# Attention passes of a graph network kernel: fewer semaphore signals from TensorE, weighing moved between the scans and fed from PSUM

## The chip, the cores and the metric

The program runs on one core of a Trainium2 chip. The core has five engines with instruction streams of their own: TensorE (PE; its weight loads are listed apart as PEld), VectorE (DVE), ScalarE (ACT), GpSimd (POOL) and SyncE (SP). They meet at semaphores: an instruction can add to one when it ends ("a signal"), and another engine's instruction can wait until it has reached a value. The metric is the time of one execution in microseconds of the device, lower is better; three runs of the kernel before took 7196.2, 7173.81 and 7191.65 us.

## The reference, cut to what matters

Four layers on a graph with 3125 nodes, 256 features and 53125 edges (25000 drawn, their reverses, and a loop at each node, sorted by destination). The first and the last sum over edges. The second is two GAT layers with 4 heads, the third is three layers of a graph transformer with 8 heads. Both do this for each edge and head (`z` or `V` is the value, `e` the score):

```python
# GAT (two layers): the score is a sum of two per-node numbers
e = leaky_relu(el[src] + er[dst], negative_slope=0.2)
ex = exp(e - segment_max(e, dst)[dst])
out = segment_sum(z[src] * (ex / segment_sum(ex, dst)[dst])[:, :, None], dst)
# graph transformer (three layers): the score is a dot product
scores = sum(Q[dst] * typed(K[src]), axis=-1) / sqrt(32) * mu[edge_type]
e = exp(scores - segment_max(scores, dst)[dst])
agg = segment_sum(V[src] * (e / segment_sum(e, dst)[dst])[..., None], dst)
```

So both need a softmax over the edges of each destination, and a sum weighted by it. Accumulations are in float32.

## The kernel before: how the work is laid out

`attend` (line 672) is called five times: twice for the GAT layers (table `tab_z`, here called the z passes; `dots` is false) and three times for the transformer layers (`tab_kv`, the kv passes; `dots` is true). It takes the sorted edges in chunks of 128 edges, one edge per partition, and 16 chunks make a window. A z pass has 28 windows, the last of them half a window, and a kv pass has 29.

The engines run the same loop over rounds, written out in Python. In round r, parts of windows r, r-1 and r-2 are worked on at once:

- **POOL** issues one indirect DMA per chunk (line 757), which gathers 128 rows of the table into a ring of four windows. Four chunks are a quad. Before a quad, POOL waits until the values that lie at its place have been used: on `s_pp`, which counts finished sums of PE, and in the kv passes on `s_mul` also (lines 748 to 753).
- **SP** loads the destinations of eight chunks at a time, broadcast over the partitions (`oht<-lo_row`, line 741), when `s_q` says that the rows they replace have been used. **ACT** makes one-hot matrices of them (L855, L858), and the other way round for the sums (L864, L869).
- **PE** `qrows` fetches the query rows by multiplying with the one-hot matrix (L785 with three bf16 terms in kv, L779 in z). `T1` (L793) transposes the window's scores; `below` (L797, L798) subtracts the maximum; `ratio` (L802) gets the factor by which earlier sums shrink; after ACT's two exponentials (L881, L882) `T5` (L807) transposes the weights back, and `factor` (L813 to L815) spreads the factor over the partitions. `agg` (L828) sums the weighted values of one unit into a PSUM buffer `pp`: a unit is one chunk in z, with six buffers, and two chunks in kv, with three.
- **DVE** `dot` and `red` make the scores in kv (L931, L936), `leaky` in z (L945, L948, L951). D1, D2, D3 are the segmented maximum, made of scans (L961 to L989). `weigh` (L1010) multiplies a quad of gathered values by the weights, `rescale` (L1000, L1001) multiplies the sum of the current tile by the factor, and `add` (L1018) adds one unit's PSUM buffer to the accumulator.
- **ACT** also copies the weights from PSUM beside the values in the ring (L886, L887, or L889 in z) and the factor to `facs` (L893); in kv it weighs the last two chunks itself (L876).

`T1`, `below`, `ratio`, `T5` and `factor` write to one PSUM bank, `pc`. Semaphores keep all other uses of that bank apart.

Four strings set the order within a round: `ORDER_V_DOTS` and `ORDER_V_SUMS` for DVE in kv and z, `ORDER_T_DOTS` and `ORDER_T_SUMS` for PE. A letter is a step and a number its part: in the V strings W0 to W3 weigh a quad of window r-2, S and R are dot and red of window r, A the adds of window r-2, P the last adds of window r-3, t the rescale, L leaky, B the residual. In the T strings C1 to C5 are T1, below, ratio, T5 and factor of window r-1, G0 to G7 the eighths of agg of window r-2, Q and N the query rows. Nothing reorders them: each engine does its list in order, and waits at its head.

The lines that the steps below refer to most:

```python
# agg, one unit: every unit signals
for c in range(UC):
    last = nc.tensor.matmul(pp[(w * NU + n) % NB][:, 0:W8], oh[...], one(w, UC * n + c, 0, W8), ...)
last.then_inc(s_pp, 1)
# weigh, one quad: values and weights both from the ring in SBUF
ex = span(w, 4 * q, c1, D, D + heads)
nc.vector.tensor_tensor(v, v, bc(ex, 3, D // heads), ALU.mult).then_inc(s_m, 1)
```

## Time and profile before

| | |
|---|---|
| median of three runs | 7191.65 us (7173.81 to 7196.2) |
| the profiled execution's own time | 7153.48 us |
| its span, first to last instruction | 7151.4 us |
| PE busy | 4511.4 us (63%) |
| DVE busy | 3873.4 us (54%) |
| ACT busy | 3586.2 us (50%) |
| POOL busy | 3942.8 us (55%) |
| TensorE clock, mean | 0.769 of full |

The profile is of one execution. "Busy" does not count waiting, branching or the issuing of ordinary DMAs, while POOL's indirect DMAs count for as long as POOL works on them. No engine is busy all the time; the page gives shares over stages of quite different kinds. The five calls of `attend` stand at 1555 to 2273, 2337 to 3052, 3236 to 3972, 4314 to 5052 and 5396 to 6138 us of the span.

### The profile page before, as it was taken

Reading aid. Unit: us, or ns where it says so; the run is one execution under the profiler, and the core shown is the slowest. Engines: PE = TensorE matmul, PEld = TensorE weight load, DVE = VectorE, ACT = ScalarE, POOL = GpSimd, SP = SyncE. Lnnn points to the kernel's source line nnn. Section 1 sums busy time; section 2 is a strip of 40 time slices with the busy share of each in tenths; the row PEclk is TensorE's granted clock in tenths of the full one; section 3 lists DMA queues with packets and bytes.
Section 4 is the critical chain, followed back from the end, with each engine's and each line's share of the span. In section 5 each row is a group of like instructions: output and inputs, shape, how many; then the busy total and the mean of one; then the engine's idle time right before and its main releaser. Section 6 shows DMA issues by size and latency. Waiting matters only on the chain. (4 is left out here: it accounts for less than half of the span.)

```text
span 7151.4 us, 82528 instructions
## 1 busy us (share of the span) xinstructions
PE 4511.4 (63%) x22100; PEld 3453.4 (48%) x22100; DVE 3873.4 (54%) x9224; ACT 3586.2 (50%) x9073; POOL 3942.8 (55%) x3964
## 2 busy tenths in 40 slices
PE   5444355445556456655777895777895777895444
PEld 3344233323444244454555784555794555673332
DVE  7222223245667356675777445777545777663223
ACT  3333132334444444455666575666575666555554
POOL 0666566647773677535666225666225666215665
PEclk9555566666777676787888997888897888997666
DMA  1111233333432433336666326666326666423333
GB/s 60 44 50 55 62 97 94 90 94 108 110 109 63 115 108 110 90 125 196 196 193 193 90 79 192 195 195 194 91 79 185 192 194 193 114 89 118 92 90 90
DMA packets 395658, 864.23 MB, mean 121 GB/s; under 512 B 93353, under 2 KB 203851, under 8 KB 391763
## 3 DMA queue, kind: packets, MB, share of 16 engines
q0 software_dynamic: 209680, 608.73, 31.4%
q1 hardware_dynamic: 177296, 246.02, 10.3%
q10 hardware_dynamic: 8243, 4.30, 0.2%
q8 instruction: 193, 3.16, 0.2%
q14 instruction: 246, 2.02, 0.1%
HBM read 743.33 MB, written 115.44 MB: 120 GB/s over the span
## 5 line engine op out<-in xcount | busy, mean ns | idle before, releaser
L757 POOL DMA_INDIRECT ring<-tab_kv,idx_i x1044 | 1072.5, 1027 | 534.2 <-issue 295.7
L757 POOL DMA_INDIRECT ring<-tab_z,src_i x880 | 948.8, 1078 | 402.0 <-issue 243.2
L1193 PE MATMUL pp<-ring,oh 128*128 128x256 f32 x1760 | 609.0, 502 | 635.8 <-issue 268.6
L1018 DVE TENSOR_TENSOR acc<-acc,pp 128x264 f32 x1576 | 668.3, 424 | 470.9 <-PE pp L828 120.7
L1327 DVE TENSOR_TENSOR acc<-acc,pp 128x256 f32 x880 | 370.5, 421 | 889.2 <-DMA tab_z<-zs 280.4
L1193 PEld LDWEIGHTS pp<-ring,oh 128*128 128x128 f32 x1760 | 416.2, 251 | 829.1 <-issue 677.3
L828 PE MATMUL pp<-ring,scratch 128*128 128x264 f32 x1760 | 678.5, 526 | 114.2 <-issue 66.7
L785 PE MATMUL pq<-Qs,oht 128*128 x4176 | 620.5, 306 | 186.4 <-issue 98.2
L828 PE MATMUL pp<-ring,X 128*128 128x264 f32 x2088 | 667.4, 454 | 51.0 <-DVE acc L1018 32.0
L1010 DVE TENSOR_TENSOR ring<-ring 128x1024 f32<-128x1024 f32 x481 | 585.9, 1219 | 187.7 <-ACT ring L889 108.6
L785 PEld LDWEIGHTS pq<-Qs,oht 128*128 128x128 bf16 x4176 | 439.3, 109 | 346.6 <-issue 238.1
L638 POOL DMA_INDIRECT rec<-R,idx_i x416 | 408.2, 981 | 274.5 <-DVE idx_i L613 142.4
L1144 POOL DMA_INDIRECT ring<-tab_y,src_i x440 | 417.9, 950 | 237.5 <-issue 123.0
L1144 POOL DMA_INDIRECT ring<-tab_h,idx_i x440 | 420.6, 956 | 224.3 <-issue 121.4
L828 PEld LDWEIGHTS pp<-ring,scratch 128*128 128x128 f32 x1760 | 401.5, 255 | 256.1 <-issue 125.2
L855 ACT ACTIVATE oht<-oht,part_c 128x1024 bf16<-128x1024 bf16 x284 | 323.3, 1138 | 401.2 <-DMA oht<-lo_row_p 197.2
L931 DVE TENSOR_TENSOR X<-ring,pq 128x1024 f32<-128x1024 f32 x261 | 317.6, 1217 | 346.7 <-issue 252.4
L828 PEld LDWEIGHTS pp<-ring,X 128*128 128x128 f32 x2088 | 423.3, 223 | 157.2 <-issue 44.3
L757 POOL DMA_INDIRECT H<-tab_kv,idx_i x348 | 351.7, 1011 | 235.0 <-issue 84.6
L864 ACT ACTIVATE X<-iota_row,lo__40877 128x128 f32<-128x128 f32 x1392 | 424.1, 388 | 2.4 <-PE pp L828 2.4
L936 DVE TENSOR_REDUCE scw<-X 128x32 f32<-128x1024 f32 x348 | 422.9, 1215 | 0.8
L1685 POOL TENSOR_TENSOR R<-H,rows 128x256 f32<-128x256 f32 x75 | 66.0, 880 | 586.1 <-DVE H L2070 586.1
(363 smaller groups left out, 9421.3 us busy)
## 6 DMA issues: line engine op xcount, KB each, us to landing
oht<-lo_row_p SPq DMA_DIRECT2D x174, 256.0 KB
oht<-lo_row_s SPq DMA_DIRECT2D x110, 256.0 KB
drow<-in_dst SPq DMA_DIRECT2D x25, 1024.0 KB
tab_h<-hs SPq DMA_DIRECT2D x25, 1024.0 KB, 4.4
tab_kv<-X SPq DMA_DIRECT2D x50, 396.0 KB, 2.7
tab_kv<-X SPq DMA_DIRECT2D x50, 384.0 KB, 3.4
ring<-tab_kv,idx_i POOLq DMA_INDIRECT x1044
ring<-tab_z,src_i POOLq DMA_INDIRECT x880
```

Source lines behind the costliest of these rows:

```text
L638: nc.gpsimd.indirect_dma_start(out=rec, out_offset=bass.IndirectOffsetOnAxis(ap=slot[:, j:j + 1], axis=0), in_=R[:, j, :], in_offset=None) ...
L757: nc.gpsimd.indirect_dma_start(out=one(w, c, 0, row), out_offset=None, in_=table, in_offset=bass.IndirectOffsetOnAxis(ap=idx[:, w * WC + c ...
L785: last = nc.tensor.matmul(o, lhs, Qs[:, bass.ds(tile_, 1), r, :].rearrange("p a d -> p (a d)"), start=(r == 0), stop=(r == 2))
L828: last = nc.tensor.matmul(pp[(w * NU + n) % NB][:, 0:W8], oh[:, w % 2, UC * n + c, :], one(w, UC * n + c, 0, W8), start=(c == 0), stop=(c ...
L855: nc.scalar.activation(oht[:, k % LOB, :], oht[:, k % LOB, :], ACT.Abs, scale=-1.0, bias=part_c[:, :]).then_inc(s_ac, 1)
L864: last = nc.scalar.activation(oh[:, w % 2, c, :], iota_row[:, :], ACT.Abs, scale=-1.0, bias=lo_s[:, w * WC + c:w * WC + c + 1])
L936: nc.vector.tensor_reduce(scw[:, w % 2, :, 4 * q:4 * q + 4].rearrange("p h c -> p c h"), prod[:, q % 2, :, :].rearrange("p c (h x) -> p c ...
L1010: nc.vector.tensor_tensor(v, v, bc(ex, 3, D // heads), ALU.mult).then_inc(s_m, 1)
L1018: nc.vector.tensor_tensor(a, a, pp[(w * NU + p) % NB][:, 0:W8], ALU.add).then_inc(s_acc, 1)
L1144: nc.gpsimd.indirect_dma_start(out=ring[:, b, k, c, :], out_offset=None, in_=table, in_offset=bass.IndirectOffsetOnAxis(ap=idx[:, 2 * p + ...
L1193: last = nc.tensor.matmul(bank[:, c * D:(c + 1) * D], oh[:, b, 2 * k + c, :], ring[:, b, k, c, :], start=True, stop=True)
L1327: nc.vector.tensor_tensor(a, a, pp[b % 2 * BP + k][:, c * D:(c + 1) * D], ALU.add).then_inc(s_v, 1)
```

## The change

It does four things, all inside `attend`:

- PE signals `s_pp` once per quad of chunks, not per unit (z: 4 per window, was 16; kv: 4, was 8). Everyone who waits on `s_pp` counts in quads: POOL before a gather, ACT before it overwrites `oh`, DVE before an `add`. In z, `s_q` is signalled once per eight query rows (2 per window, was 4). The signal behind `T5` goes, since `factor` now comes right after it and signals for both. In all a whole window has 9 signals of PE in z (was 24) and 11 in kv (was 16).
- `factor` no longer waits until ACT has copied the weights, and ACT copies the factor in the same step as the weights.
- `weigh` reads its weights from the PSUM bank `pc`, where `T5` left them. ACT still copies them to the ring, since the sums need them there.
- The four orders are changed. DVE weighs only after D1 (and so after `T1` of the next window), with all four parts before D3 (which lets `below` overwrite the bank). PE's aggregation comes later in the round.

```diff
-    ORDER_V_DOTS = order("W0 S0 P6 R0 W1 P7 S1 t D1 A0 R1 D2 A1 W2 D3 A2 S2 W3 R2 A3 S3 A4 R3 A5")
+    ORDER_V_DOTS = order("S0 P6 R0 P7 t D1 W0 S1 W1 R1 D2 W2 A0 W3 D3 S2 A1 R2 A2 A3 S3 A4 R3 A5")
-    ORDER_T_SUMS = order("l G0 C1 G1 Q0 Q1 G2 Q2 Q3 G3 G4 C2 C3 G5 C4 G6 C5 G7")
+    ORDER_T_SUMS = order("l C1 Q0 Q1 Q2 Q3 G0 G1 G2 G3 G4 C2 C3 G5 C4 C5 G6 G7")
...
-                            e.wait_ge(s_q, 2 * (k - LOB + 1))
+                            e.wait_ge(s_q, (2 if dots else 1) * (k - LOB + 1))
...
-                                e.wait_ge(s_pp, (w + 3 - RW) * NU + QU * (q + 1))
+                                e.wait_ge(s_pp, (w + 3 - RW) * NQ + q + 1)
                             elif w >= RW:
-                                e.wait_ge(s_pp, (w + 2 - RW) * NU + QU * (q + 1))
+                                e.wait_ge(s_pp, (w + 2 - RW) * NQ + q + 1)
...
-                        last.then_inc(s_q, 1)
+                        if dots or q % 2:
+                            last.then_inc(s_q, 1)
...
-                        nc.tensor.transpose(ex_t, S1, ident[:, :]).then_inc(s_T5, 1)
+                        nc.tensor.transpose(ex_t, S1, ident[:, :])
 
                     def factor(w):
-                        e.wait_ge(s_ex, w + 1)
                         e.wait_ge(s_oh, 2 * w + 1)
...
-                        last.then_inc(s_pp, 1)
+                        if n % QU == QU - 1:
+                            last.then_inc(s_pp, 1)
...
                     def rows(w, h):
-                        e.wait_ge(s_pp, w * NU + HU * (h + 1))
+                        e.wait_ge(s_pp, w * NQ + NQ // 2 * (h + 1))
...
-                        e.wait_ge(s_T5, w + 1)
+                        e.wait_ge(s_fac, w + 1)
                         ex = ex_t.rearrange("p (h c) -> p c h", h=HD)
...
                             nc.scalar.copy(span(w, 0, WC, D, W8), ex).then_inc(s_ex, 1)
-
-                    def factors(w):
-                        e.wait_ge(s_fac, w + 1)
                         nc.scalar.copy(facs[:, w % 2, :], fac).then_inc(s_fc, 1)
...
-                        if r >= 2:
-                            factors(r - 2)
...
                         if q == 0:
                             e.wait_ge(s_ex, w + 1)
+                            e.wait_ge(s_fc, w + 1)
...
-                        ex = span(w, 4 * q, c1, D, D + heads)
+                        ex = ex_t.rearrange("p (h c) -> p c h", h=HD)[:, 4 * q:c1, 0:heads]
...
-                        e.wait_ge(s_pp, w * NU + (p + 1 + 2 * NU))
+                        e.wait_ge(s_pp, (w + 2) * NQ + p // QU + 1)
```

Some lines of `attend` move up by three or four: L807 becomes L808, L893 becomes L891, L931 becomes L927, L1010 becomes L1007, L1018 becomes L1015.

On PE, in a z round, at the end of the softmax of window r-1. Before (L807 is T5, L813 to L815 factor, L828 agg with its buffers pp, L793 T1 of the next round):

```order
L807 MATMUL pc<-ident,scratch 128x128
L828 MATMUL pp_12540<-ring,scratch 128x264
L828 MATMUL pp_12541<-ring,scratch 128x264
L813 MATMUL pc<-one_r 128x8
L814 MATMUL pc<-neg_r,scratch 128x8
L815 MATMUL pc<-gr,scratch 128x8
L828 MATMUL pp_12542<-ring,scratch 128x264
L828 MATMUL pp_12543<-ring,scratch 128x264
L660 TENSOR_LOAD tile__4185
L828 MATMUL pp_12544<-ring,scratch 128x264
```

And after the change (L808 is T5, L794 T1):

```order
L808 MATMUL pc<-ident,scratch 128x128
L813 MATMUL pc<-one_r 128x8
L814 MATMUL pc<-neg_r,scratch 128x8
L815 MATMUL pc<-gr,scratch 128x8
L828 MATMUL pp_12540<-ring,scratch 128x264
L828 MATMUL pp_12541<-ring,scratch 128x264
L828 MATMUL pp_12542<-ring,scratch 128x264
L828 MATMUL pp_12543<-ring,scratch 128x264
L660 TENSOR_LOAD tile__4185
L794 MATMUL pc<-ident,scw 128x128
```

Factor has moved ahead of two units of agg, directly behind T5, and the next round opens with T1 and not with agg.

On DVE, at the start of a kv round, before (L1010 weighs, L931 is dot, L936 red, L1018 add, L660 and the ISA rows fetch addresses, L1000 begins the rescale):

```order
L1010 TENSOR_TENSOR ring<-ring 128x4x256
L931 TENSOR_TENSOR X<-ring,pq_42872 128x1024
L1018 ISA
L1018 TENSOR_TENSOR acc<-acc,pp_42876 128x264
L936 TENSOR_REDUCE scw<-X 128x4x8
L1010 TENSOR_TENSOR ring<-ring 128x4x256
L1018 ISA
L1018 TENSOR_TENSOR acc<-acc,pp_42874 128x264
L931 TENSOR_TENSOR X<-ring,pq_42873 128x1024
L660 TENSOR_LOAD tile__40876
L1000 ISA
```

After the change, from the rescale of the same round on (L996, L997 rescale, L957 and L958 are the scans of D1, L1007 weighs, L927 is dot, L932 red):

```order
L996 TENSOR_TENSOR acc<-acc,facs 128x256
L997 ISA
L997 TENSOR_TENSOR acc<-acc,facs 128x8
L957 SCALAR_TENSOR_TENSOR X<-pen,pc 128x128
L958 SCALAR_TENSOR_TENSOR X<-pen,pc 128x128
L1007 TENSOR_TENSOR ring<-ring,pc 128x4x256
L927 TENSOR_TENSOR X<-ring,pq_42815 128x1024
L1007 TENSOR_TENSOR ring<-ring,pc 128x4x256
L932 TENSOR_REDUCE scw<-X 128x4x8
```

Weighing has gone from the head of the round to behind D1, and `pc` in PSUM stands among what it reads.

## Rows read from the trace of the kernel before

**Rows 1.** Busy by stretch: PE, PEld, DVE, ACT, POOL; clock, DMA share, GB/s.

```profile
1640.80:2220.80 580.00, 351.30 (x1481) 247.23 (x1481) 363.92 (x928) 283.22 (x625) 410.25 (x375) 0.73 0.41 109
2220.80:2273.20 52.40, 41.56 (x163) 27.32 (x164) 43.65 (x112) 21.33 (x60) 2.52 (x2) 0.81 0.11 10
3297.60:3911.30 613.70, 463.80 (x2368) 343.33 (x2367) 471.43 (x873) 381.22 (x1076) 409.11 (x399) 0.83 0.68 196
```

**Rows 2.** The factor's copy L893, once per window, in the z stretch.

```profile
L893 ACT COPY facs<-pc x25: 165/165/166, 1640.8 to 2220.8; 128x8 f32<-128x8 f32 x25
```

**Rows 3.** The same copy in the kv stretch.

```profile
L893 ACT COPY facs<-pc x26: 165/165/167, 3297.6 to 3911.3; 128x8 f32<-128x8 f32 x26
```

**Rows 4.** Groups of instructions, z stretch 1640.8 to 2220.8: busy, mean ns, idle before.

```profile
L757 POOL DMA_INDIRECT ring<-tab_z,src_i x375 | 411.0, 1096 | 173.7 <-issue 102.5 <-remote 41.4 <-PE pp L828 29.9
...
L1018 DVE TENSOR_TENSOR acc<-acc,pp 128x264 f32 x379 | 161.4, 426 | 107.1 <-remote 45.9 <-issue 21.9 <-PE pp L828 20.1
...
L1010 DVE TENSOR_TENSOR ring<-ring 128x1024 f32<-128x1024 f32 x94 | 114.7, 1220 | 76.1 <-ACT ring L889 65.7 <-issue 10.4
```

**Rows 5.** Groups on DVE, kv stretch 3297.6 to 3911.3.

```profile
L931 DVE TENSOR_TENSOR X<-ring,pq 128x1024 f32<-128x1024 f32 x75 | 91.2, 1217 | 63.1 <-issue 63.1
L1018 DVE TENSOR_TENSOR acc<-acc,pp 128x264 f32 x197 | 83.1, 422 | 76.8 <-DMA keep_link<-link_p 50.9 <-PE pp L828 21.6 <-issue 4.0
```

**Rows 6.** Timeline of a z window: start, duration, idle before.

```profile
1811.74 0.20 PE L802 MATMUL pc<-G,one_c 128*1 128x8 f32 x2
1811.87 1.16 PE L828 MATMUL pp<-ring,scratch 128*128 128x264 f32 x4
...
1815.52 0.43 DVE L1018 TENSOR_TENSOR acc<-acc,pp 128x264 f32 x1 [2.02 <-remote]
...
1818.39 0.43 DVE L1018 TENSOR_TENSOR acc<-acc,pp 128x264 f32 x1 [2.44 <-issue]
...
1823.97 0.28 ACT L881 ACTIVATE scratch<-pc 128x128 f32<-128x128 f32 x1 [7.42 <-remote]
```

**Rows 7.** Timeline at the end of a z pass, gathers over.

```profile
2269.21 0.20 PE L802 MATMUL pc<-G,one_c 128*1 128x8 f32 x2
...
2269.45 0.28 ACT L881 ACTIVATE scratch<-pc 128x128 f32<-128x128 f32 x1 [10.11 <-PE pc L802]
```

**Rows 8.** Timeline of a kv window.

```profile
3433.08 0.20 PE L802 MATMUL pc<-G,one_c 128*1 128x8 f32 x2
3433.21 2.13 PE L828 MATMUL pp<-ring,X 128*128 128x264 f32 x4
...
3435.11 0.95 POOL L757 DMA_INDIRECT ring<-tab_kv,idx_i  x1 [0.30 <-issue]
...
3437.86 0.32 SPq L741 DMA_DIRECT2D oht<-lo_row_p  x1
3438.00 0.28 ACT L881 ACTIVATE X<-pc 128x128 f32<-128x128 f32 x1 [2.82 <-remote]
3438.04 0.43 DVE L1018 TENSOR_TENSOR acc<-acc,pp 128x264 f32 x1 [0.50 <-DMA keep_link<-link_p]
```

**Rows 9.** The page, gathers of all passes: busy, mean ns, idle before.

```profile
L757 POOL DMA_INDIRECT ring<-tab_kv,idx_i x1044 | 1072.5, 1027 | 534.2 <-issue 295.7
L757 POOL DMA_INDIRECT ring<-tab_z,src_i x880 | 948.8, 1078 | 402.0 <-issue 243.2
...
L1144 POOL DMA_INDIRECT ring<-tab_y,src_i x440 | 417.9, 950 | 237.5 <-issue 123.0
```

**Rows 10.** Timeline, a gather beside a weighing.

```profile
3407.74 1.22 DVE L1010 TENSOR_TENSOR ring<-ring 128x1024 f32<-128x1024 f32 x1
3408.26 1.51 POOL L757 DMA_INDIRECT ring<-tab_kv,idx_i  x1 [0.30 <-issue]
```

**Rows 11.** Timeline, factor and the query rows behind it, kv.

```profile
3463.06 0.38 PE L813 MATMUL pc<-one_r 1*128 1x8 f32 x2 [0.30 <-issue]
...
3463.82 1.48 PE L785 MATMUL pq<-Qs,oht 128*128 x12
```

More of the change, by code:

```diff
@@ L666, in order @@
         return [(x[0], int(x[1:] or 0)) for x in text.split()]
-    ORDER_V_DOTS = order("W0 S0 P6 R0 W1 P7 S1 t D1 A0 R1 D2 A1 W2 D3 A2 S2 W3 R2 A3 S3 A4 R3 A5")
-    ORDER_V_SUMS = order("W0 P10 P11 W1 P12 P13 W2 P14 P15 t D1 A0 A1 D2 A2 A3 D3 A4 A5 W3 B A6 A7 A8 A9 L")
-    ORDER_T_DOTS = order("l C1 G0 Q2 G1 G2 Q3 G3 C2 C3 G4 C4 G5 C5 N0 G6 N1 G7")
-    ORDER_T_SUMS = order("l G0 C1 G1 Q0 Q1 G2 Q2 Q3 G3 G4 C2 C3 G5 C4 G6 C5 G7")
+    ORDER_V_DOTS = order("S0 P6 R0 P7 t D1 W0 S1 W1 R1 D2 W2 A0 W3 D3 S2 A1 R2 A2 A3 S3 A4 R3 A5")
+    ORDER_V_SUMS = order("P12 P13 P14 P15 t D1 W0 W1 D2 A0 A1 W2 A2 A3 W3 D3 A4 A5 B A6 A7 L A8 A9 A10 A11")
+    ORDER_T_DOTS = order("l C1 Q2 G0 G1 Q3 G2 G3 C2 C3 G4 C4 C5 N0 G5 G6 N1 G7")
+    ORDER_T_SUMS = order("l C1 Q0 Q1 Q2 Q3 G0 G1 G2 G3 G4 C2 C3 G5 C4 C5 G6 G7")
     def attend(Qs, heads, row, at_k, idx, table, scratch, lay, plus=None):
@@ L724, in attend @@
             ratio_row, fac = pc[0:1, 3 * P:3 * P + HD], pc[:, 3 * P + HD:3 * P + 2 * HD]
-            (s_go, s_oh, s_ev, s_q, s_mul, s_red, s_T1, s_G, s_Gm, s_eg, s_T5, s_fac, s_fc, s_ex, s_m, s_pp,
+            (s_go, s_oh, s_ev, s_q, s_mul, s_red, s_T1, s_G, s_Gm, s_eg, s_fac, s_fc, s_ex, s_m, s_pp,
              s_acc, s_d, s_ma, s_ab, s_ac, s_max) = (s.sem(n) for n in (
-                 "go", "oh", "ev", "q", "mul", "red", "T1", "G", "Gm", "eg", "T5", "fac", "fc", "ex", "m", "pp",
+                 "go", "oh", "ev", "q", "mul", "red", "T1", "G", "Gm", "eg", "fac", "fc", "ex", "m", "pp",
                  "acc", "d", "ma", "ab", "ac", "max"))
@@ L763, in _ @@
                 def _(e):
-                    e.sem_inc(s_pp, 2 * NU)
+                    e.sem_inc(s_pp, 2 * NQ)
                     def tiles(w):
@@ L942, in leaky @@
                             e.wait_ge(s_g[w % RW][q], 64 * (w // RW + 1))
-                        e.wait_ge(s_q, w * NQ + quads(w))
+                        e.wait_ge(s_q, 2 * w + quads(w) // 2)
                         sc = scw[:, w % 2, :, :]
```

## The prediction, written before the changed kernel ran

> **What bounds the kernel now.** I read the table of busy time by stretch first, for the five attention passes [rows 1]. The z passes run at 580.0 / 24 = 24.2 us a window (the factor is copied 25 times between the ends, [rows 2]), the kv passes at 613.7 / 25 = 24.5 us [rows 3]. No engine fills that. Per window DVE is busy 363.92 / 24 = 15.2 us in z and 471.43 / 25 = 18.9 us in kv, PE 14.6 and 18.6. POOL must issue 16 gathers; one takes 0.95 us where nothing disturbs it and the next starts 0.30 us later [rows 8, 10], so it can't be under 16 x 1.25 = 20.0 us. Where a z pass has no gathers left, three windows take 52.4 us, 17.5 each [rows 1]. So POOL's 20.0 us are the floor of a window, and the passes stand 4.1 (z) and 4.5 us (kv) above it.
>
> The groups by line say where DVE stands idle. In z: 65.7 us before the weighing L1010, for ACT's copy of the weights, and 45.9 + 20.1 = 66.0 us before the adds, for PE; together 131.7 / 24 = 5.5 us a window [rows 4]. In kv: 63.1 us before the product L931 and 50.9 + 21.6 = 72.5 us before the adds; 135.6 / 25 = 5.4 us [rows 5]. Names such as keep_link or remote are no clue, since nothing is loaded there: these waits are for PE's semaphores, or in kv partly for gathered rows.
>
> The timeline then shows that PE is not late, its signals are. In a z window ratio (L802) ends at 1811.94, and the exponential that waits for it starts at 1823.97, though ACT had been idle 7.42 us; the adds at 1815.52 and 1818.39 waited 2.02 and 2.44 us while PE had finished every unit by 1813.03 [rows 6]. At the end of the pass, with no gathers, the same step takes 2269.45 - 2269.41 = 0.04 us [rows 7]. In a kv window ratio ends at 3433.28 and agg at 3435.34; POOL's last gather before a pause ends at 3436.06, and then SP, ACT and DVE all start between 3437.86 and 3438.04 on signals of PE [rows 8]. I read it so: while gathers are landing, PE's signals can be held back in a queue, pass it one by one some 2.9 us apart (1815.52 to 1818.39), and all get out when the DMA goes quiet. In the z example ratio's signal stood behind those of the units summed before it, one per unit.
>
> **The change part by part.** *Fewer signals.* z gives 9 a window instead of 24, kv 11 instead of 16. What I can price is the waiting of DVE above, as if it shrank with the number in the queue: z 15/24 x 5.5 = 3.4 us a window, kv 5/16 x 5.4 = 1.7. Bounds: nothing, if the hold does not depend on the number; the floor of POOL, 4.1 and 4.5, if it goes altogether. I take 3.0 in z, a little less than the share, since a POOL that pauses less also leaves the queue fewer quiet moments, and 1.6 in kv.
>
> *Counting in quads* makes consumers wait for later units: in z the first add of a quad for three more units of 1.16 / 2 = 0.58 us or less [rows 6], 1.7 us. In z DVE has W2, D2 and other work between a quad's weighing and its adds, and 4.8 us to spare up to POOL's 20.0 (15.2 busy), so I count nothing; bounds 0 and 1.7. In kv it is one unit, 2.13 us at the slow clock [rows 8], and DVE has 1.1 us to spare up to 20.0; bounds 0 and 2.1, in the 1.6 above I left 0.1 for it.
>
> *Weighing after D1.* DVE executes the same instructions, so its busy time stays. The wait of 65.7 / 24 = 2.7 us before the weighing in z [rows 4] loses its place at the head of the round: the last adds, the rescale and both scans of D1 now come first, over 1.7 us of work (four adds at 0.43, then the others). The rescale needs the factor, which ACT now copies with the weights, so part of the wait moves to it. This is inside the 3.0. What queues behind the weighing now is agg, and POOL behind agg: in kv quad 0 is summed some 5 us later in DVE's round. A gather is issued a round ahead of its dot, so I count nothing, and keep the price for a rival.
>
> *Weights from PSUM.* An add or a product with one operand in PSUM takes what one with both in SBUF takes: L931 1217 ns against L1010 1220 for the same 1024 elements [rows 4, 5]. So no time on DVE. On POOL there is a gain. Gathers average 1078 ns in z and 1027 in kv, but 950 in the stage without weighing [rows 9], and a long one (1.51 us) starts inside a weighing [rows 10]. That stage has DVE adds with one operand in PSUM (L1327) all along, so such an operand does not lengthen a gather; I take it that two operands in SBUF do. If all of the excess goes, that is 16 x 0.128 = 2.0 us a window in z and 16 x 0.077 = 1.2 in kv on POOL. POOL itself waits (41.4 + 29.9 us in z, 3.0 a window [rows 4]), so this time largely turns into waiting for PE unless the signals are faster; it is what lets the 3.0 and 1.6 be reached, and I do not add it.
>
> *T5 and factor in one.* ACT waits for 0.76 us more of PE (L813 to the query rows, 3463.06 to 3463.82 [rows 11]) before it copies the weights, and PE no longer waits for that copy before factor. In both kinds of pass the next user is a round head away; nothing either way, bounds -0.5 and +0.8.
>
> One rule speaks against the PSUM operand. By the Trainium skill (VectorE: DVE Perf Modes, the TRN2 errata) a DVE instruction with a PSUM source has 120 cycles of fixed cost where one from SBUF has 58, 65 ns more; with four weighings in 48 + 75 windows that would be an estimated 32 us of DVE time. The rows of L931 and L1010 show no such difference, so I go by them.
>
> **The sum.** 24 windows in each of two z passes and 25 in each of three kv passes run at the steady rate; the last windows without gathers have prompt signals already. 48 x 3.0 = 144 us and 75 x 1.6 = 120 us, together 264. The profiled execution took 7153.48 us, 2.1 us more than its span, and would come to 6889. The median of the runs is 38.2 us above it, so 7191.65 - 264 = 6928 us.
>
> **The rivals.** *Floor:* the hold nearly vanishes, since it grows only when signals come faster than they get out, and POOL runs without a pause: 48 x 4.1 + 75 x 4.5 = 534 us at most, with 0.8 us a window kept for start and end of waits about 436, so 6756 us. For it: the release in steps [rows 6]; against: in kv 11 signals in 20 us are still one in 1.8 us, more than one in 2.9.
>
> *Only the port:* the hold does not depend on the number of signals, and only the shorter gathers count. 48 x 2.0 + 75 x 1.2 = 186 us if all of it is on the path, half of it since POOL waits anyway: about 93, 7099 us. For it: in kv everything was let go at once when the DMA went quiet, whatever stood in the queue [rows 8]. By the Trainium skill (Advanced Engine Details and Errata, DMA Bandwidth Details) a semaphore increment costs about one cycle, and then fewer of them are worth nothing and this rival would be the outcome; the 12 us of rows 6 do not look like one cycle.
>
> *Slower:* the hold stays, and meets a kv round with less slack. The fifth add now needs a unit that PE sums after factor and twelve query matmuls, 0.76 + 1.48 = 2.24 us later [rows 11], and the weighing of quad 0 comes some 5 us later, so that POOL's turn on PE comes sooner in a hold. If a kv window loses the 2.24 us that DVE's order no longer covers and z gains only the 0.5 us of shorter gathers, that is 75 x 2.24 - 48 x 0.5 = 144 us, 7336 us. It decides once the signals in kv are held longer than about 2 us as often as now. For it: kv has little to spare in DVE (18.9 of 20.0).
>
> **How the numbers follow.** The sum as it stands 0.60, with a range of its own of 6830 to 7030; the floor 0.17; only the port 0.10; slower 0.13, most of it near the middle between no change and 7336. A change under 0.3% (22 us) is what a measurement can't tell from none. Faster by more: 0.60 + 0.17 + 0.10, less 0.02 for a weak port, 0.85; within 0.3%: 0.05; slower: 0.10. The range reaches into the floor on one side and over the port case on the other: 6760 to 7170 us.
>
> **What would show it.** In the profile after: 24.2 us a window in z falls to about 21.2 and 24.5 in kv to about 22.9; the gathers average about 950 to 960 ns in both; the wait before the weighing in z (65.7 us) falls to a quarter or less, and the exponential after ratio starts within 3 us of it in most z windows. DVE's weighing stays at 1.22 us. Wrong it would be if kv windows get longer, if gathers stay over 1.03 us, or if the waits for adds stay at 2.7 us a window with the signals halved.

## The result and the profile after

The changed kernel takes 7396.55 us (median of four, 7387.9 to 7402.4), the kernel before 7182.73 us on the same chip. The ratio is 1.0304, 95% interval 1.0286 to 1.0322: 3% slower. The prediction said 6928 us, 0.965. Measured again beside other runs of the kernel before (h1_after below) the ratio was 1.0303.

Busy time by stretch of the profile after; columns as in [rows 1]. The first line runs from the first to the 25th copy of the factor (24 windows) of the first z pass, the second is the end of that pass, without gathers, the third the 25 windows of the first kv pass.

```profile
1642.90:2305.90 663.00, 356.80 (x1488) 246.05 (x1488) 369.79 (x931) 281.69 (x626) 360.84 (x376) 0.73 0.35 96
2306.80:2364.30 57.50, 38.75 (x151) 27.49 (x151) 42.70 (x107) 20.07 (x56) 0.00 (x0) 0.79 0.03 3
3492.60:4117.30 624.70, 459.62 (x2353) 338.95 (x2352) 470.07 (x870) 378.77 (x1077) 374.02 (x394) 0.82 0.67 190
```

A z window takes 663.0 / 24 = 27.6 us where it took 24.2 [rows 1], a kv window 624.7 / 25 = 25.0 where it took 24.5. DVE is as busy as before, POOL is 49 us less busy in z (360.8 against 410.3) and yet the stretch is 83 us longer. From the first to the last copy of the factor the two z passes grew by 89 and 91 us, the three kv passes by 14, 16 and 8: 218 of the 249 us by which the profiled span grew (7400.7 against 7151.4), and 180 of them in z. At the end of the pass, where nothing is gathered, the round is longer too: 57.5 us where nearly the same stretch took 52.4 [rows 1].

The gathers on the page after, to be read beside [rows 9]:

```profile
L757 POOL DMA_INDIRECT ring<-tab_kv,idx_i x1044 | 993.0, 951 | 775.2 <-issue 288.8
L757 POOL DMA_INDIRECT ring<-tab_z,src_i x880 | 844.0, 959 | 663.3 <-PE pp L828 263.4
...
L1141 POOL DMA_INDIRECT ring<-tab_y,src_i x440 | 418.0, 950 | 239.3 <-issue 122.8
...
L757 POOL DMA_INDIRECT H<-tab_kv,idx_i x348 | 329.6, 947 | 127.5 <-issue 103.3
```

They average 947 to 959 ns, as forecast, but POOL's idle time before z gathers rose from 402.0 to 663.3 us. The groups by line of the z stretch say for what the engines wait (busy, mean ns, idle before; beside [rows 4]):

```profile
L1015 DVE TENSOR_TENSOR acc<-acc,pp 128x264 f32 x380 | 162.6, 428 | 263.3 <-DMA keep_link<-link_p 172.3 <-issue 50.1 <-DVE acc L1015 40.7
L1007 DVE TENSOR_TENSOR ring<-ring,pc 128x1024 f32<-128x1024 f32 x96 | 114.1, 1209 | 0.0
...
L757 POOL DMA_INDIRECT ring<-tab_z,src_i x376 | 360.8, 960 | 304.0 <-PE pp L828 128.6 <-issue 105.6 <-DMA keep_link<-link_p 69.8
...
L890 ACT COPY ring<-pc 128x128 f32<-128x128 f32 x25 | 6.6, 265 | 184.5 <-remote 136.6 <-issue 45.6 <-PE pc L815 2.3
```

The wait before the weighing is gone (76.1 to 0.0), and the adds wait 263.3 us where they waited 107.1: together 11.0 us a window against 183.2 / 24 = 7.6. POOL waits 128.6 us for agg where it waited 29.9. ACT waits 7.7 us a window (184.5 / 24) for the factor. In kv the wait moved in the same way: 63.1 us before the product and 76.8 before the adds [rows 5] became 7.7 and 142.4:

```profile
L927 DVE TENSOR_TENSOR X<-ring,pq 128x1024 f32<-128x1024 f32 x75 | 91.0, 1214 | 7.7 <-DMA ab<-in_L_gnn_ar 7.7
L1015 DVE TENSOR_TENSOR acc<-acc,pp 128x264 f32 x196 | 82.9, 423 | 142.4 <-remote 128.0 <-issue 6.5 <-PE pp L828 5.8
```

The timeline of one z round of after: start, duration, idle before.

```profile
1883.86 0.36 PE L815 MATMUL pc<-gr,scratch 1*128 1x8 f32 x2
1884.15 2.53 PE L828 MATMUL pp<-ring,scratch 128*128 128x264 f32 x8
1886.77 0.43 DVE L1015 TENSOR_TENSOR acc<-acc,pp 128x264 f32 x1 [0.21 <-issue]
1889.55 0.27 ACT L890 COPY ring<-pc 128x128 f32<-128x128 f32 x1 [6.92 <-remote]
1891.38 0.95 POOL L757 DMA_INDIRECT ring<-tab_z,src_i  x1 [0.30 <-issue]
...
1894.74 0.43 DVE L1015 TENSOR_TENSOR acc<-acc,pp 128x264 f32 x1 [7.54 <-DMA keep_link<-link_p]
1894.75 0.80 SPq L741 DMA_DIRECT2D oht<-lo_row_s  x2
...
1895.39 0.95 POOL L757 DMA_INDIRECT ring<-tab_z,src_i  x1 [3.06 <-DMA keep_link<-link_p]
...
1898.36 0.43 DVE L996 TENSOR_TENSOR acc<-acc,facs 128x256 f32 x1 [0.91 <-DVE acc L1015]
...
1898.78 0.41 DVE L957 TENSOR_TENSOR_SCAN scratch<-pen,pc 128x128 f32<-128x128 bf16 x1
...
1899.42 2.32 DVE L1007 TENSOR_TENSOR ring<-ring,pc 128x1024 f32<-128x1024 f32 x2
...
1900.87 5.46 PE L828 MATMUL pp<-ring,scratch 128*128 128x264 f32 x16 [8.58 <-issue]
...
1904.49 0.43 DVE L1015 TENSOR_TENSOR acc<-acc,pp 128x264 f32 x1 [1.36 <-issue]
1905.19 0.94 POOL L757 DMA_INDIRECT ring<-tab_z,src_i  x1 [5.10 <-PE pp L828]
```

Read it as a chain. The factor (L815) ends at 1884.22 and the last units of quad 3 (L828) at 1886.68. POOL is in a run of twelve gathers that ends at 1892.33. Two signals are late, and they do not get out together. The factor's is 5.3 us late and gets out in the middle of POOL's run, at 1889.55. That of quad 3 is 8 us late and gets out at 1894.74, 2.4 us after POOL's last gather. It is the second that decides: only now can DVE add quad 3, rescale, do D1 and weigh, and PE start agg, at 1900.87, while the factor had been copied long before the rescale began (1898.36). POOL, which got four more gathers with quad 3, has nothing left by 1900.1 and stands 5.10 us for agg of quad 0. So in each round POOL issues twelve gathers, pauses 3 us, issues four, and pauses 5 us.

I call a signal held when the reader stands idle though the work behind the signal has ended. In all 24 windows of this stretch the factor's signal is held, by 0.69 to 6.74 us, and DVE stands 2.07 to 7.88 us, 7.3 in the mean, before the first add that needs quad 3. The exponential behind ratio starts 0.04 us after it in all 24 windows, though POOL gathers then too; before, it was held in 12 of 24. So the signal that [rows 6] show held now comes through, and others are held in its place.

### The profile page after: what moved, and what is told of

It reads as the page before. It is cut to its first block and busy times, and to the rows that moved or that the text cites. A ratio compares the mean times of both kernels' runs of the same rounds, so it can differ in the third digit from the quotient of the medians.

```text
span 7400.7 us, 82528 instructions
## 1 busy us (share of the span) xinstructions
PE 4504.7 (61%) x22100; PEld 3461.5 (47%) x22100; DVE 3885.9 (53%) x9224; ACT 3576.8 (48%) x9073; POOL 3736.3 (50%) x3964
## 3 DMA queue, kind: packets, MB, share of 16 engines
q1 hardware_dynamic: 177296, 246.02, 10.1%
## 5 line engine op out<-in xcount | busy, mean ns | idle before, releaser
L757 POOL DMA_INDIRECT ring<-tab_kv,idx_i x1044 | 993.0, 951 | 775.2 <-issue 288.8
L1015 DVE TENSOR_TENSOR acc<-acc,pp 128x264 f32 x1576 | 671.6, 426 | 1056.1 <-DMA keep_link<-link_p 349.6
L757 POOL DMA_INDIRECT ring<-tab_z,src_i x880 | 844.0, 959 | 663.3 <-PE pp L828 263.4
L1190 PE MATMUL pp<-ring,oh 128*128 128x256 f32 x1760 | 590.7, 496 | 662.3 <-DVE acc L1324 232.2
L828 PE MATMUL pp<-ring,scratch 128*128 128x264 f32 x1760 | 602.1, 489 | 451.7 <-DVE ring L1007 373.5
L828 PE MATMUL pp<-ring,X 128*128 128x264 f32 x2088 | 673.0, 466 | 295.5 <-DVE ring L1007 143.2
L785 PE MATMUL pq<-Qs,oht 128*128 x4176 | 648.7, 317 | 188.1 <-DVE X L927 114.2
L828 PEld LDWEIGHTS pp<-ring,scratch 128*128 128x128 f32 x1760 | 385.4, 238 | 610.3 <-issue 497.4
L828 PEld LDWEIGHTS pp<-ring,X 128*128 128x128 f32 x2088 | 444.4, 229 | 432.5 <-issue 306.0
L785 PEld LDWEIGHTS pq<-Qs,oht 128*128 128x128 bf16 x4176 | 459.4, 112 | 354.7 <-issue 234.8
L1007 DVE TENSOR_TENSOR ring<-ring,pc 128x1024 f32<-128x1024 f32 x481 | 576.0, 1209 | 0.0
L932 DVE TENSOR_REDUCE scw<-X 128x32 f32<-128x1024 f32 x348 | 422.5, 1214 | 0.9
L757 POOL DMA_INDIRECT H<-tab_kv,idx_i x348 | 329.6, 947 | 127.5 <-issue 103.3
L927 DVE TENSOR_TENSOR X<-ring,pq 128x1024 f32<-128x1024 f32 x261 | 316.8, 1214 | 128.7 <-DMA ab<-in_L_gnn_ar 69.2
```

The lines of the kernel that those rows point to most:

```text
L757: nc.gpsimd.indirect_dma_start(out=one(w, c, 0, row), out_offset=None, in_=table, in_offset=bass.IndirectOffsetOnAxis(ap=idx[:, w * WC + c ...
L785: last = nc.tensor.matmul(o, lhs, Qs[:, bass.ds(tile_, 1), r, :].rearrange("p a d -> p (a d)"), start=(r == 0), stop=(r == 2))
L828: last = nc.tensor.matmul(pp[(w * NU + n) % NB][:, 0:W8], oh[:, w % 2, UC * n + c, :], one(w, UC * n + c, 0, W8), start=(c == 0), stop=(c ...
L932: nc.vector.tensor_reduce(scw[:, w % 2, :, 4 * q:4 * q + 4].rearrange("p h c -> p c h"), prod[:, q % 2, :, :].rearrange("p c (h x) -> p c ...
L1015: nc.vector.tensor_tensor(a, a, pp[(w * NU + p) % NB][:, 0:W8], ALU.add).then_inc(s_acc, 1)
L1190: last = nc.tensor.matmul(bank[:, c * D:(c + 1) * D], oh[:, b, 2 * k + c, :], ring[:, b, k, c, :], start=True, stop=True)
```

## The experiments

All ratios are to the kernel before on the same chip. The window times come from each profile: the first to the 25th (z) or 26th (kv) copy of the factor, mean over the two z and the three kv passes.

| kernel | ratio (95%) | z us | kv us |
|---|---|---|---|
| before | 1 | 24.1 | 24.6 |
| after | 1.0304 (1.0286 to 1.0322) | 27.6 | 24.9 |
| e1 z as before | 1.0048 (1.0032 to 1.0065) | 24.4 | 24.8 |
| e2 only fewer signals | 0.9978 (0.9966 to 0.9990) | 23.9 | 24.4 |
| e3 only the orders | 1.0207 (1.0190 to 1.0224) | 24.4 | 25.6 |
| e4 after, old signals | 1.0163 (1.0146 to 1.0180) | 25.8 | 24.7 |
| e5 after, weights from SBUF | 1.0084 (1.0058 to 1.0111) | 24.0 | 24.8 |
| e6 after, z weighs first | 1.0048 (1.0029 to 1.0067) | 23.8 | 24.4 |
| e7 and kv weighs first | 1.0281 (1.0255 to 1.0307) | 23.8 | 26.6 |
| e8 before, half the bytes | 1.0039 (1.0020 to 1.0057) | 24.6 | 24.5 |
| f1 after, more POOL work | 1.0263 (1.0245 to 1.0282) | 26.8 | 24.6 |
| f2 e6 with SBUF weights | 1.0116 (1.0098 to 1.0134) | 24.6 | 24.6 |
| f3 e2 and T5 with factor | 1.0024 (1.0009 to 1.0039) | 24.8 | 24.2 |
| f4 before, more signals | 0.9988 (0.9976 to 1.0000) | 24.5 | 24.4 |
| h1 after again | 1.0303 (1.0281 to 1.0324) | 27.6 | 24.8 |
| h2 after, late two from SBUF | 1.0088 (1.0065 to 1.0111) | 24.3 | 24.7 |
| h3 best of each | 1.0014 (1.0000 to 1.0029) | 24.0 | 24.6 |

Two profiles of after agree within 0.1 us a window (h1 and after), but kernels that take the same time can differ by 0.4 us (f4 and before in z), so small differences are read from the ratios. The runs g1, g2 and g3, made under another condition, stand further below.

**Where the loss is.** e1_sums_old takes the two z passes back to before.

> The two z passes as before (orders, one signal per unit, query signal per four rows, T5 with a signal of its own, factor copied in the next round, weights read from the ring), the three kv passes as after. Read from the two traces, the change costs the z passes about 90 us each and the kv passes 8 to 15 us each. If the passes are independent, this kernel takes 7183 + 35 = 7218 us (7200 to 7235), under both theories below; a time near 7300 or more would say that kv loses more than its trace shows.

Measured 1.0048, 7206.83 us: kv costs 34 us, z the rest. The passes are independent, as was expected.

**Number of signals.** e2_signals_only is the kernel before with

```diff
-                        last.then_inc(s_pp, 1)
+                        if n % QU == QU - 1:
+                            last.then_inc(s_pp, 1)
```

and its waits in quads. f4_more_signals is the kernel before with

```diff
                         last.then_inc(s_pp, 1)
+                        e.sem_inc(s_xx, 1)
```

> Before with fewer signals alone: units counted in quads in all five passes, query rows of z signalled per eight; orders, T5, factor and weights in SBUF stay as before. Theory order (the loss comes from the new order of the round, which puts weighing, and so agg and the POOL waits behind it, later): no loss here, 6950 to 7180 us, whatever the shorter hold gives. Theory quads (adds and gathers wait for the last unit of a quad, and that costs more than the hold gives back): slower than before, 7250 to 7400 us, all of it in z where a quad is four units.

> Before with one more signal of PE behind every unit of agg, on a semaphore for which nobody waits: 16 more a window in z (24 become 40), 8 more in kv (16 become 24). Theory number (the prediction's: signals pass one by one while gathers land, so the hold grows with their number): waits of 5.5 us grow by two thirds in z and by half in kv, 48 x 3.7 + 75 x 2.7 = 380 us, ratio 1.03 to 1.06. Theory burst (the hold ends when POOL's run of gathers ends, whatever is queued): ratio 0.998 to 1.004.

Fewer signals gain 0.2% (10 a window in z instead of 24), and 16 more a window cost nothing. The groups of the z stretch of e2 show where the wait went (L1029 is the add, L1021 the weighing):

```profile
L1029 DVE TENSOR_TENSOR acc<-acc,pp 128x264 f32 x378 | 161.0, 426 | 177.3 <-remote 122.6 <-issue 28.0 <-DVE acc L1029 23.4
L1021 DVE TENSOR_TENSOR ring<-ring 128x1024 f32<-128x1024 f32 x93 | 113.3, 1219 | 0.9 <-issue 0.7
```

Before, 107.1 and 76.1 [rows 4], 183.2 in all; now 177.3 and 0.9. The weighing no longer waits, the adds do, and the sum has hardly moved; in f4 it is 101.4 + 92.0 = 193.4 us with 40 signals a window. The hold did not grow or shrink with the number, as it would in a queue that drains one signal at a time. One reservation: the signals that f4 adds are instructions of their own on a semaphore for which nobody waits, and no run shows that they go the way of those behind a matmul.

**Bytes.** e8_half_rows halves what a gather fetches, from the fifth window on; it leaves out the right half of each row, and only its time counts.

```diff
+                                k = row if w < RW else row // 2
...
-                                    out=one(w, c, 0, row), out_offset=None, in_=table,
+                                    out=one(w, c, 0, k), out_offset=None,
+                                    in_=table if w < RW else table.rearrange("n (a b) -> (n a) b", a=2),
```

> Before with half the bytes per gather: from the fifth window of every pass on, each gather fetches rows of half the width (132 of 264, 260 of 520 values) into the left half of its place; the right half keeps older rows, so values are wrong and only the time counts. The number of gathers, their descriptors, all signals and orders are as before. Theory traffic (PE's signals stand behind the gathers' bytes): the hold halves, DVE's 5.5 us a window of waiting fall to about 2.8, and 48 + 75 windows give back 330 us: 6850 us (6750 to 7000). Theory issue (the hold goes with POOL's issuing, whatever the bytes): 7140 to 7200 us.

1.0039, with 66 GB/s in the z stretch where before has 109, and DVE's waits before the adds and the weighing are 84.5 + 102.1 = 186.6 us: halving the bytes does not shorten the hold. The number of gathers was the same, so this does not tell POOL's issuing from the landing of gathers.

**The parts of the change.** e3_orders_only puts after's four orders into the kernel before; e4_unit_signals takes the signals of after back to one per unit, and to one per four query rows in z; f3_signals_factor adds the merged T5 and factor to e2; e5_sbuf_weights is after with

```diff
-                        ex = ex_t.rearrange("p (h c) -> p c h", h=HD)[:, 4 * q:c1, 0:heads]
+                        ex = span(w, 4 * q, c1, D, D + heads)
```

> Before with the four new orders alone: every signal stays (one per unit, one per four query rows, T5), weights in SBUF. Theory order: z loses some 3 us a window as in the end of the pass without gathers (20.5 against 17.5 us), 48 x 3 = 144 us, and with kv's 35 it is 7330 to 7400 us. Theory quads: 7150 to 7220 us.

> After with one signal per unit again in all passes, and a query signal per four rows in z; new orders, T5 and factor merged and weights in PSUM stay. Theory order: no gain from taking the quads away; 7380 to 7500 us, since more signals are held. Theory quads: back to 7183 or below with the gathers' shorter issue, 7050 to 7230 us.

> Before with fewer signals (as e2_signals_only) and with T5 and factor in one as well: T5's signal is dropped, ACT copies weights and factor together. Orders as before, weights from SBUF. I expect nothing from this edit: within 0.3% of e2_signals_only, ratio to before 0.995 to 1.001. Rival: the factor's own signal was often held (ACT waited up to 4.3 us a window for it), and merging it gives 1 us a window in z: 0.985 to 0.993.

> After with the weighing's second operand read from the ring in SBUF, as before; nothing else is changed (new orders, quads, T5 and factor merged). Expected on POOL: gathers that run beside a weighing are long again, so their mean goes from 0.96 us back to about 1.05. The orders alone took 7320 us and after with unit signals 7295, so weights from PSUM and the merged factor are worth 25 us at most: 7397 + 25 = 7420 us (7390 to 7450) if POOL's time is on the path; under the rival that POOL has idle time for it, within 0.1% of after.

One path through them adds the parts one by one: signals 0.9978, then T5 and factor 1.0024, then the orders 1.0084 (e5), then the weights from PSUM 1.0304. So the parts are -0.2, +0.5, +0.6 and +2.2%, along this path; another order of the edits would share them out in another way, as e3 and e4 show. In f3 the order of z is the old one, where agg of one eighth stands between T5 and factor, so merging makes ACT wait for that too; in after it does not stand there. e5 went against both of its theories: I had 7420 us or no change, and it is 2.2% below after. e3 and e4 fit neither of theirs: the orders alone cost 2.1%, mostly in kv (25.6 us a window) and not in z as the theory had it, 10 us below its range, and quads cost 1.4% in the orders of after (1.0304 against 1.0163) while they gain 0.2% in the old ones. The page of e5 has the long gathers back:

```profile
L757 POOL DMA_INDIRECT ring<-tab_kv,idx_i x1044 | 1024.9, 982 | 629.9 <-issue 296.0
...
L757 POOL DMA_INDIRECT ring<-tab_z,src_i x880 | 910.1, 1034 | 426.3 <-issue 249.6
```

66 us more work in the z gathers than after (910.1 against 844.0), 237 us less idle before them. In e5 the factor's signal is held in none of the 24 windows (its copy starts 0.04 us behind it), and DVE stands 0.4 us in the mean before the first add of quad 3, where after has 7.3. POOL issues sixteen gathers in one run, with no pause over 1 us.

**Not the operand, its place.** e6_weigh_first moves D1 and two weighings ahead of the four adds in z, and the other two weighings each a place forward; f2_weigh_first_sbuf is the same with weights from SBUF; e7_weigh_first_all does it in kv too.

```diff
-    ORDER_V_SUMS = order("P12 P13 P14 P15 t D1 W0 W1 D2 A0 A1 W2 A2 A3 W3 D3 ...
+    ORDER_V_SUMS = order("D1 W0 W1 P12 P13 P14 P15 t D2 W2 A0 A1 W3 D3 A2 A3 ...
```

> After with the z order of DVE changed: D1 W0 W1 at the head of the round and the four adds P12 to P15 behind them, W2 and W3 each a place earlier; all signals, quads, PSUM weights as after. Theory order (weighing behind the four adds makes agg late, and the first add of the round meets quad 3 just after PE issued it): the two weighings cover quad 3, agg can start earlier, and z returns to the length it has with quads in the old order; 7397 - 180 = 7217 us, a little less for the shorter gathers, so 7150 to 7230. Rival (the held signals cost what they cost wherever DVE meets them in the new set of signals): no return, 7320 us or more.

> The z order D1 W0 W1 P12 to P15 of e6_weigh_first, with weights read from the ring in SBUF instead of PSUM; all else as there. If an operand in PSUM costs DVE or PE by itself, this is faster than e6_weigh_first (ratio to before 1.0048) by the 2% by which e5_sbuf_weights was faster than after: 0.985. If the phase theory holds, the price of 2% belongs to the order of after alone, and here the longer gathers are worth little, between 0.3% less and 0.8% more: 1.002 to 1.013.

> As e6_weigh_first, and in kv as well D1 and W0 directly behind the first product, the adds P6 and P7 behind W0 and R0, and A0 behind the rescale as before. Theory order: kv gets its 35 us back too, so 35 us below e6_weigh_first, 7110 to 7200 us. Rival: D1 so early waits for T1's own held signal, and kv is no shorter or longer: e6_weigh_first plus 0 to 100 us.

e6 is at 1.0048, 2.5% below after with every other edit kept, and here the PSUM operand gains: 0.7% less than f2. So an operand in PSUM does not cost by itself, and f2 lies where the theory had it (1.002 to 1.013) and not at 0.985. DVE does not take longer over it either (1209 ns). The timeline of an e6 round:

```profile
1892.74 0.95 POOL L757 DMA_INDIRECT ring<-tab_z,src_i  x1 [0.30 <-issue]
...
1892.82 0.33 PE L794 MATMUL pc<-ident,scw 128*128 128x128 f32 x1 [1.84 <-issue]
...
1895.41 0.42 DVE L957 TENSOR_TENSOR_SCAN scratch<-pen,pc 128x128 f32<-128x128 bf16 x1 [4.78 <-DMA oh<-rec,map_i]
...
1896.06 1.20 DVE L1007 TENSOR_TENSOR ring<-ring,pc 128x1024 f32<-128x1024 f32 x1
1896.10 1.13 ACT L856 ACTIVATE oht<-oht,part_c 128x1024 bf16<-128x1024 bf16 x1
1896.13 0.94 POOL L757 DMA_INDIRECT ring<-tab_z,src_i  x1 [2.45 <-DMA keep_link<-link_p]
```

A signal is held there too: T1 (L794) ends at 1893.15, D1 waits until 1895.41, 1.7 us after POOL's last gather (1893.69); over the stretch DVE waits 145.8 us before D1, and only 65.2 before the adds. But W0 follows 0.65 us later and not 4.7 (1894.74 to 1899.42), and POOL has work again at once. In kv the same move is a miss: e7 was to take 7110 to 7200 us and took 7339, with 26.6 us a window and the adds of the first kv pass waiting 178.7 us where after has 142.4. T1's signal was not the cause, since D1 (L957) waits 4.5 us in 25 windows; what was stays open.

```profile
L1015 DVE TENSOR_TENSOR acc<-acc,pp 128x264 f32 x196 | 83.0, 423 | 178.7 <-PE pp L828 106.5 <-issue 61.1 <-remote 11.1
...
L957 DVE TENSOR_TENSOR_SCAN X<-pen,pc 128x128 f32<-128x128 bf16 x25 | 10.5, 421 | 4.5 <-issue 2.1 <-PE pc L794 1.2
```

**More work for POOL.** f1_paced lets POOL clear an unused buffer before each z quad.

```diff
+                            if not dots:
+                                if w or q:
+                                    e.wait_ge(s_id, w * NQ + q)
+                                nc.gpsimd.memset(idle[:, :], 0.0).then_inc(s_id, 1)
```

> After with more work for POOL: in the z passes it clears a buffer of 128x264 that nothing reads (324 to 351 ns in the rows of other such fills) before the four gathers of each quad, 1.3 us a window. Nothing else is changed. Theory phase (weights from PSUM only shorten the gathers, and with shorter gathers a z round locks so that the signal of quad 3 and the factor's are caught by the same burst of POOL): the longer turn of POOL moves the round out of that lock, and z falls from 27.7 toward the 24.3 us of the version with weights in SBUF, total ratio to before 1.005 to 1.02, faster than after in spite of more work. Theory load (POOL is part of the path, the operand in PSUM costs by itself): 48 x 1.3 = 62 us more, ratio 1.035 to 1.042.

```profile
L761 POOL MEMSET idle<- 128x264 f32 x94 | 30.8, 328 | 136.1 <-PE pp L834 90.9 <-remote 45.2
```

With 1.3 us more to do in a window z is 0.8 us shorter, ratio 1.0263 against 1.0304. More work made it faster, which speaks against POOL's load. The sign is the phase theory's, the size is not: the round did not leave its long cycle. The factor's signal is still held in 20 of 24 windows, by 2.2 us in the mean where after has 5.3, and the wait before the first add of quad 3 is 5.5 us where after has 7.3.

**Which weighing.** h2_late_two_sbuf is after with W2 and W3 alone reading SBUF.

```diff
+                        if q >= 2:
+                            ex = span(w, 4 * q, c1, D, D + heads)
```

> The variant of g1_late_two_sbuf once more. Without holds 0.992 again. With holds, if W2 and W3 must lengthen the gathers beside them to keep the round out of the long cycle: 1.008 to 1.015; if W0 and W1 decide, 1.025 to 1.031.

> The changed kernel as it is, beside the kernel before on one chip. Where signals are held (before near 7150 us) it takes 3.0% more as measured already. Where they are not (before near 6431 us): theory hold (the whole loss comes from signals caught by POOL's run, the new order is sound without them) faster than before, near the variants with two weighings each way, 0.985 to 0.992. Theory structure (z loses 3 us a window by its order alone, as in the end of the pass without gathers): 48 x 3 = 144 us, ratio 1.015 to 1.025.

h2 is at 1.0088 beside 1.0303 for after on the same chip: two weighings of four read from SBUF take back nearly all of the 2.2%, and not half of it. The opposite pair was not run in this condition, so it is not shown that it must be these two. Groups of its z stretch of 585.4 us:

```profile
L757 POOL DMA_INDIRECT ring<-tab_z,src_i x375 | 378.3, 1009 | 209.7 <-issue 107.7 <-PE pp L828 77.1 <-DMA keep_link<-link_p 24.8
...
L856 ACT ACTIVATE oht<-oht,part_c 128x1024 bf16<-128x1024 bf16 x48 | 54.7, 1140 | 266.8 <-DMA oht<-lo_row_s 266.8
...
L890 ACT COPY ring<-pc 128x128 f32<-128x128 f32 x25 | 6.6, 265 | 53.1 <-PE pc L815 23.2 <-remote 19.3 <-issue 10.6
```

The wait for the factor is 53.1 us where after has 184.5 (58.3 in e5), and ACT waits 266.8 us for SP's loads, which wait for the signal of the query rows. The timeline, in the middle of a run of sixteen gathers:

```profile
1900.47 0.36 PE L815 MATMUL pc<-gr,scratch 1*128 1x8 f32 x2
...
1900.77 3.32 PE L828 MATMUL pp<-ring,scratch 128*128 128x264 f32 x8
1900.79 0.95 POOL L757 DMA_INDIRECT ring<-tab_z,src_i  x1 [0.30 <-issue]
1900.87 0.27 ACT L890 COPY ring<-pc 128x128 f32<-128x128 f32 x1 [1.18 <-issue]
...
1906.43 0.43 DVE L1017 TENSOR_TENSOR acc<-acc,pp 128x264 f32 x1 [4.13 <-DMA keep_link<-link_p]
```

The factor's signal takes 0.04 us, here and in all 24 windows, with the same instructions on PE and POOL gathering as in after. That of quad 3 is 2.3 us late (1904.09 to 1906.43), and DVE stands 0.8 us in the mean before it. So other signals are held, and that of the query rows can be late at little price, since the window takes 24.3 us. In after it is that of quad 3, on which DVE, PE and POOL all hang.

**Without holds.** In three runs the kernel before, made beside them, took 6431.35 us (6421.35 to 6435.69, seven runs) instead of some 7150. The record names chip 7 for them and also for e5 to e8, where before took 7142.58 us. g1_late_two_sbuf is the kernel of h2, g2_early_two_sbuf has the condition `q < 2`, g3_best_of_each is the kernel of h3: z as e6, kv as f3.

> After with the weighings W2 and W3 of each window reading their weights from SBUF, W0 and W1 from PSUM as in after. W2 and W3 stand where POOL runs the gathers of quads 0 to 2, so if it is these that must be long to keep POOL behind (so that it is still busy when quad 3's signal is given, and the hold doesn't fall on the head of the round), z goes back to about 24.3 us and the ratio to before is 1.008 to 1.015. If W0 and W1 decide, it stays at 1.025 to 1.031.

> The reverse: W0 and W1 read their weights from SBUF, W2 and W3 from PSUM. In the long cycle of after POOL has four gathers in hand while W0 and W1 run and then stands idle for 5 us, so making these four longer costs nothing and gives nothing: 1.025 to 1.031 if W2 and W3 decide, 1.008 to 1.015 if W0 and W1 do. If both runs give half of the gain, the sum of the lengths counts and not the place.

> z passes as in e6_weigh_first (23.9 us a window in its trace), kv passes as in f3_signals_factor (24.3 us; old kv orders, two units a signal, T5 and factor merged, weights from SBUF). If the passes are independent, against before (24.3 and 24.9): 48 x 0.4 + 75 x 0.55 = 60 us less by the traces, ratio 0.992; from the ratios of the two parents by the same traces 0.997 to 1.001. I take 0.996.

> The variant of g3_best_of_each once more (z weighing first from PSUM, kv in its old orders with two units a signal). Without holds 0.987 again. With holds, from the windows of its two parents, 0.992 to 1.001; I take 0.997.

There the ratios are 0.9919 (0.9899 to 0.9938), 0.9906 (0.9890 to 0.9923) and 0.9873 (0.9856 to 0.9889), so none of them tells what it was made to tell, but something else: the kernel of h2, which loses 0.9% with holds, gains 0.8% without them. The timeline of g1, in the middle of POOL's gathers:

```profile
1906.24 0.20 PE L803 MATMUL pc<-G,one_c 128*1 128x8 f32 x2
...
1906.47 0.28 ACT L882 ACTIVATE scratch<-pc 128x128 f32<-128x128 f32 x1 [5.17 <-PE pc L803]
...
1907.53 0.95 POOL L757 DMA_INDIRECT ring<-tab_z,src_i  x1 [0.30 <-PE pp L828]
...
1908.03 0.36 PE L815 MATMUL pc<-gr,scratch 1*128 1x8 f32 x2
...
1908.42 0.27 ACT L890 COPY ring<-pc 128x128 f32<-128x128 f32 x1 [1.63 <-PE pc L815]
```

Ratio's signal tells nothing here, as it is as prompt in after; but the factor's arrives within 0.04 us in all 24 windows, gathers on both sides, and DVE stands 0.2 us before the first add of quad 3. In its z stretch POOL waits 10.1 us for PE in 24 windows, and a window takes 21.7 us in z and 21.1 in kv:

```profile
L757 POOL DMA_INDIRECT ring<-tab_z,src_i x387 | 402.5, 1040 | 118.0 <-issue 107.9 <-PE pp L828 10.1
```

So whether signals are held while gathers run depends on a condition outside the program, and the kernel before takes some 700 us less without it. How much of this is the holds is not shown: between the profiles of h2 and g1, the same kernel, the five passes explain 400 of 846 us, and the other stages were not read. The two kinds of profile differ in one thing more. Their pages give a time from issue to landing for the gathers without holds (g1, first line) and none with holds (h2, second line):

```profile
ring<-tab_z,src_i POOLq DMA_INDIRECT x880, 2.8
...
ring<-tab_z,src_i POOLq DMA_INDIRECT x880
```

The trace of h2 also holds fewer semaphore updates (37273 against 86321 in g1). No run tells whether the recording takes part in the hold.

h3 shows that the gain of the best version is there only without holds: 0.9873 becomes 1.0014, just outside the 0.992 to 1.001 that I had expected. Its kv windows take 24.6 us and not the 24.2 of f3, so the two halves did not simply add. With holds only e2 (0.9978) and, within its interval no different from before, f4 (0.9988) are below 1. How after itself does without holds was not measured.

## Why the prediction was wrong

**What held.** The reading that PE is not late and its signals are [rows 6 to 8] was right. The gathers came to 947 to 959 ns, DVE's weighing to 1209, the wait before the weighing vanished, and the exponential follows ratio at once. That two operands in SBUF lengthen a gather and one in PSUM does not holds too: in before the 270 z gathers that overlap a weighing take 1366 ns in the mean and the 601 others 951, in after the 192 that overlap one take 947. The Trainium skill (SBUF — State Buffer, "SBUF: two separate sides") says that a DVE instruction with two SBUF inputs and a GpSimd one that reads SBUF exclude each other. The direction agrees; that the second waits for the whole of the first no run shows. The prediction also cited 65 ns more for a PSUM source, by the Trainium skill (VectorE: DVE Perf Modes, the TRN2 errata). It did not show (1209 against 1214 to 1220 ns; in h2, in one trace, 1203 with the weights in PSUM against 1219).

**First failed step: the price of a signal.** "z 15/24 x 5.5 = 3.4 us a window", with 264 us in sum, all that the forecast gains. e2 gives 16 us, and its z waits are 178.2 us against 183.2. My bound "nothing, if the hold does not depend on the number" was the truth. I had read from [rows 6] that signals come out one by one some 2.9 us apart. That was one pair of adds. The next two stand 1.4 us apart, and POOL's gathers go on through all four but for one pause of 1.3 us:

```profile
1819.82 0.43 DVE L1018 TENSOR_TENSOR acc<-acc,pp 128x264 f32 x1 [1.00 <-remote]
...
1821.23 0.43 DVE L1018 TENSOR_TENSOR acc<-acc,pp 128x264 f32 x1 [0.98 <-remote]
```

Nor does a held signal always wait until the gathers pause, as I had read from [rows 8]: the factor's signal of after gets out in the middle of a run in 23 of 24 windows. On the number alone the one-cycle increment of the Trainium skill (Advanced Engine Details and Errata, DMA Bandwidth Details) fits e2 and f4. The 8 us by which a single signal is late in after are another matter.

**Second failed step, and the one that turned the sign: shorter gathers can't hurt.** I gave the PSUM operand a worth of 0 to 2.0 us a window and no loss. It cost 2.2%: 27.6 - 24.0 = 3.6 us a window in z between after and e5. With shorter gathers POOL's runs fall otherwise, and the signals of the factor and of quad 3 are held in all 24 windows; in e5 the factor's is held in none and quad 3's, by over 1 us, in 3. In e6's order the same operand gains 0.7%. A range that goes below nothing there would have been right. POOL's idle time of 3.0 us a window, which I had on record, said only that a faster POOL need not gain.

**Third: counting in quads and weighing after D1, both priced at nothing in z.** Each costs nothing or little alone: quads in the old order take 23.9 us a window, the new orders alone 24.4, quads and the new order with SBUF weights 24.0. Together with PSUM weights they take 27.6, and 25.8 with a signal per unit, so quads cost 1.8 us there: P12 is now DVE's first work of the round and needs the unit that PE sums last, and behind it stand the rescale, D1, the weighing, agg and POOL. I had named that queue and priced it only for kv.

**T5 and factor.** Predicted nothing, bounds -0.5 and +0.8 us. Between e2 and f3 it is +0.5% in total, +0.8 us a window in z and -0.2 in kv: inside the bounds, at their upper end in z.

**The rival "slower"** (7336 us, 0.13) had the right side, by luck: its 144 us came from the wrong place. kv lost 0.3 us a window and not 2.24, z lost 3.5 where it was to gain 0.5, and 214 us were measured. The forecast's own tests said it: kv windows got longer, and the waits for adds rose to 11.0 us a window.

**Open.** How the length of a weighing's gathers decides which signals are held is only argued; no run moves a single gather, and of the two pairs of weighings only one was tried with holds. What holds the signals, why some given during a run pass in 0.04 us, and why there was no hold in g1 to g3, no run tells.

## What to carry to other kernels

Where a wait moves to the next consumer when it is removed (183 to 178 us here), ask what ends it, not how many stand in it. Put behind a wait for a signal that can be late only what nobody else waits for: the same edits cost 3.0% with four adds and a rescale before the weighing and 0.5% with the weighing first. And test a schedule edit in both orders; where signals are held while another engine works, making that engine faster can cost 2% in one order and gain 0.7% in another.

## What the runs showed of the hardware

- PE's signals can reach DVE, ACT, POOL and SP 5 to 8 us late while POOL issues indirect gathers (5.3 and 8 us in the round of after). Some get out in the middle of POOL's run (1889.55), others 1.7 to 2.4 us after its last gather (1893.69 to 1895.41 in e6, 1892.33 to 1894.74 in after). Others given in such a run take 0.04 us: ratio's in all 24 windows of after, the factor's in all 24 of h2 and e5. Half the bytes (1.0039) and more signals (0.9988) leave the time as it is.
- In one set of runs the same kernels showed no hold (0.04 us from L815 to its copy in g1), and the kernel before took 6431 us instead of some 7150.
- An indirect gather on POOL takes 947 ns in the mean beside a DVE product with one operand in PSUM (after) and 951 beside none (before), and 1366 in z beside one with both operands in SBUF (before).
- The DVE product itself takes 1203 ns with one operand in PSUM and 1219 with both in SBUF (h2).
